# A group-normalised displaced convolution: sums as four lane tiles inside the row products, matrices written in place, one TensorE loop

## The chip, the cores and the metric

One core of one Trainium2 chip. The time is device microseconds of one execution. An execution under the profiler gives the trace; it took 1213.86 us, of which the trace's span, from the first to the last instruction, is 1212.0 us. The TensorE clock granted over it was 0.996 of full speed.

## The reference

The input x is [32 images, 384 channels, 64, 64] in float32. It is normalised over groups of 12 channels of one image, and each channel is then displaced by whole pixels and convolved with a 5x5 Gaussian of its own sub-pixel shift; 48 positions of 8 channels share an offset. The result is added to x:

```
gn(v): g = v.reshape(B, 32, 12, H, W); (g - mean(g)) / sqrt(var(g) + 1e-5)
disp = gn(x) shifted by round(offset[p]), zeros outside
kw   = exp(-|d + (offset - round(offset))|^2 / 0.5) on 5x5, normalised to sum 1
out  = x + conv_depthwise(disp, kw, padding=2)
```

Shift and Gaussian are separable, so one position is two 64x64 matrices: ay over rows and ax over columns.

## The kernel before, in words

The 384 channels are 16 superblocks of 24 channels (two groups, three positions of eight). A superblock is 16 steps of two images; a step holds 2 x 24 planes. On the 128 partitions lie four lanes of 32: each lane is one channel of a set of four, and its 32 partitions are 16 blocks of 4 rows for each of the 2 images. There are 256 steps, in 128 pairs.

Per step:

- SyncE loads the step into one of 16 slots of `xin` once the slot's old result is stored.
- VectorE takes statistics (L444, six per pair), GpSimd turns them into summands (L260, L262), TensorE multiplies them by a matrix of ones to sum over partitions (L599, `sum_stats`, once per pair), VectorE reduces the sums (L451, `sums`), and GpSimd makes the coefficients rstd and bias (L277 to L288). This runs two pairs (LEAD) ahead of the use.
- ACT (L543) and GpSimd (L297) normalise half of a step each into `norm`, double buffered.
- TensorE makes the row products (L607, `y_product`): for each of the 3 positions and 4 rows, four concurrent products of 32x128 tiles, one per lane, into PSUM. `ps` has two halves v of four banks; a lane has its bank, and columns 0 to 383 of it are used.
- ACT copies them out of PSUM into `y` (L552).
- TensorE makes the column products (L618, `x_products`) of 64x64 tiles, back into the same half of `ps`.
- VectorE adds them to `xin` (L463 and L466), and ACT issues the two stores (L569) two steps later.

In float32 a matmul of the program appears in the trace as two loads and two matmuls.

The order of the work is written out by hand for each engine. On TensorE a pair is `two_steps` (L629): row products of the even step for positions 1 and 2 (position 0 was begun at the end of the last pair, `begin_even`, L624), row products of the odd step, column products of the even step, the sums of pair p+2 into columns 384 and up of bank 3 of half 0, column products of the odd step, and position 0 of the next even step. It is a loop over 126 pairs (L674); the last two pairs follow as written-out code (L676) without sums. The other engines run `step` for the first superblock as written-out code, a loop over 14, and the last written out again.

The matrices of the next superblock are made during the current one: distances on GpSimd (L235, L241), squares and exponentials on ACT (L522, L526), the mask on VectorE (L418, `values`, at step 11), then `next_ay` by ACT in two strided activations of 768 elements (L533, at step 13) and `next_ax` by GpSimd (L249, at step 12). VectorE copies `next_ay` into `ay` ahead of the adds of step 14, once all row products of the superblock are done (`swap_rows`, L423: three copies), and `next_ax` into `ax` in step 15 (`swap_columns`, L430).

Semaphores count steps: a wait of TensorE for `norm0_ready`, `y_ready`, `result0_ready` and so on asks for a step's number, which is the loop's register `one` plus 0, 1 or 2.

Of the kernel before, what the change touches and what calls it, by code (L numbers as in the profile page):

```python
# [11 lines left out]
P = 128  # L12
# [33 lines left out]
def displaced_conv(nc: bass.Bass, x: bass.AP, offset: bass.AP, out: bass.AP):  # L46
# [7 lines left out]
    with ExitStack() as ctx:  # L54
# [25 lines left out]
        next_ay = sb("next_ay", [P, POS, R, P])  # L80
# [42 lines left out]
        next_ax = sb("next_ax", [P, POS, HW])  # L123
# [39 lines left out]
        next_ax_ready = sem("next_ax_ready")  # L163
        next_ay_ready = sem("next_ay_ready")
# [45 lines left out]
        def _(pool):  # L210
# [34 lines left out]
            def column_matrices(c):  # L245
                pool.wait_ge(made, c + 1)
                if c is not 0:
                    pool.wait_ge(ax_ready, STEPS * c)
                pool.tensor_tensor(next_ax[:], t_msk[:, :, R, :],  # L249
                                   gain[:, bass.ds(POS * c, POS)].unsqueeze(2).to_broadcast([P, POS, HW]),  # L250
                                   ALU.mult).then_inc(next_ax_ready, 1)
# [58 lines left out]
            coefficients(1, 1, early=True, used=False)  # L310

            def step(c, s, head, tail):
# [3 lines left out]
                if not (tail and s // PAIR + LEAD >= STEPS // PAIR):  # L316
# [14 lines left out]
        def _(dve):  # L331
# [80 lines left out]
            def values(c):  # L412

                dve.wait_ge(exp_ready, c + 1)
                if c is not 0:
                    dve.wait_ge(next_ax_ready, c)
                    dve.wait_ge(next_ay_ready, B * c)
# [4 lines left out]

            def swap_rows(c):  # L423
                if c is not 0:
                    dve.wait_ge(y_done, STEPS * c)
                dve.wait_ge(next_ay_ready, B * (c + 1))  # L426
                for k in range(POS):
                    nc.vector.tensor_copy(ay[:, k], next_ay[:, k]).then_inc(mats_ready[k], STEPS)  # L428

            def swap_columns(c):  # L430
                dve.wait_ge(next_ax_ready, c + 1)
                if c is not 0:
                    dve.wait_ge(x_done, ADDS * STEPS * c)
                nc.vector.tensor_copy(ax[:], next_ax[:]).then_inc(ax_ready, STEPS)
# [12 lines left out]
            def sums(pair, v, early=False, read=False):  # L447
# [27 lines left out]
            nc.vector.engine_nop().then_inc(result1_ready, SPARE)  # L475
# [8 lines left out]
            swap_columns(0)  # L484
            swap_rows(0)
            sums(1, 1, early=True)
            for s in range(2 * PAIR, AHEAD):
                all_statistics(s)

            def step(c, s, head, tail):  # L490
                t, p = STEPS * c + s, STEPS // PAIR * c + s // PAIR
                if s == STEPS - PAIR and not tail:
                    swap_rows(c + 1)
                for part in range(ADDS):
                    add_x(t, s, part)
                if s % PAIR == 0:
                    if not (tail and s // PAIR + LEAD >= STEPS // PAIR):
                        sums(p + LEAD, (s // PAIR + LEAD) % 2, read=True)
                else:
                    if s == STEPS - 1 and not tail:  # L500
                        swap_columns(c + 1)
                    if not (tail and s + AHEAD >= STEPS):
                        for f in (s - 1 + AHEAD, s + AHEAD):
                            statistics(c + f // STEPS, f % STEPS, 0, p + AHEAD // PAIR if f % PAIR == 0 else None)
                            statistics(c + f // STEPS, f % STEPS, 1)
                            statistics(c + f // STEPS, f % STEPS, 2)
# [5 lines left out]
        def _(act):  # L512
# [15 lines left out]
            def fill_rows(c, part):  # L528
                if part == 0:
                    act.wait_ge(made, c + 1)  # L530
                    if c is not 0:
                        act.wait_ge(mats_ready[POS - 1], STEPS * c)
                nc.scalar.activation(next_ay[:].rearrange("p n r (m b) -> p n (r m) b", b=B)[:, :, :, part],  # L533
                                     t_msk[:, :, 0:R].rearrange("p n r m -> p n (r m)"), ACT.Identity,
                                     scale=same[:, part:part + 1]).then_inc(next_ay_ready, 1)
# [24 lines left out]
            for part in range(B):  # L560
                fill_rows(0, part)
            for s in range(PAIR):
                normalise(s, s, 0, True)
# [7 lines left out]
            def step(c, s, head, tail):  # L571
# [4 lines left out]
                elif not head:  # L576
                    store(c - 1, s - BEHIND + STEPS, t - BEHIND)
                if not (tail and s + PAIR >= STEPS):
                    normalise(t + PAIR, (s + PAIR) % STEPS, STEPS // PAIR * c + (s + PAIR) // PAIR, False)
                if not tail:  # L580
# [6 lines left out]
                    if s == 13:  # L587
                        for part in range(B):
                            fill_rows(c + 1, part)
            run(step)  # L590
            for s in range(STEPS - BEHIND, STEPS):
# [3 lines left out]
        def _(pe):  # L595


            def sum_stats():
                nc.tensor.matmul(ps[:, 0, 3, SUMS], ones[:, :],  # L599
                                 summands[:].rearrange("p t n s -> p (t n s)"),  # L600
                                 start=True, stop=True).then_inc(stat_summed, 1)
# [27 lines left out]
            def two_steps(one, more=True, last=False):  # L629

                two, three = one + 1, one + 2
                if not isinstance(one, int):
                    two, three = pe.snap(two), pe.snap(three)
# [24 lines left out]
                if not last:  # L658

                    pe.wait_ge(result0_ready, two)  # L660
                    pe.wait_ge(result1_ready, two)
                    if more:
                        pe.wait_ge(sums_ready, one)
                    begin_even(three)
# [34 lines left out]
```

## Time and profile before

| | |
|---|---|
| median of 3 runs | 1213.13 us (1212.42 to 1213.94) |
| profiled execution | 1213.86 us |
| its span | 1212.0 us |
| TensorE busy, matmuls | 1168.3 us, 96% |
| VectorE busy | 995.4 us, 82% |
| ACT busy | 697.8 us, 58% |
| GpSimd busy | 661.0 us, 55% |
| HBM read and written | 402.7 MB, 332 GB/s over the span |

Busy time is the sum over an engine's instructions, and matmuls overlap, so 96% does not say how well TensorE is used; it says that it hardly ever has nothing in it. For the order of events the timeline is the view: each row has a start, a length, an engine and a line of the code. The chain of waits tells which engine the end hung on.

### The profile page before, as it was taken

How to read it: one execution, taken by the hardware profiler on the slowest of the kernel's cores; microseconds unless marked ns; L12 is line 12 of the kernel's file. 1: busy time of each engine (PE TensorE's matmuls, PEld its weight loads, DVE VectorE, ACT ScalarE, POOL GpSimd, SP SyncE). 2: the span in 40 equal slices, each digit the busy share in tenths (PEclk: the TensorE clock that was granted, in tenths of full speed). 3: DMA queues.
4: the chain of work that ended last, by engine and by line, in shares of the span. 5: the costliest groups of instructions: out<-in, count | busy, mean ns of one | idle time of the engine just before them, and what ended most of it. 6: DMA issues, size and time to landing. Idle time of an engine off the chain costs nothing.

```text
span 1212.0 us, 110760 instructions
## 1 busy us (share of the span) xinstructions
PE 1168.3 (96%) x49408; PEld 1126.2 (93%) x49408; DVE 995.4 (82%) x1530; ACT 697.8 (58%) x595; POOL 661.0 (55%) x1478
## 2 busy tenths in 40 slices
PE   2999999999999999999999999999999999999996
PEld 2899999999999999999999999999999999999996
DVE  7688887887888888788888888888888888878863
ACT  3466656656556555655656655565665665556553
POOL 5455656455565555555556555555655556565551
PEclk9999999999999999999999999999999999999999
DMA  6999999999999999999999999999999999999955
GB/s 210 333 356 349 346 347 345 344 339 350 337 347 346 335 351 346 341 346 344 344 340 350 341 337 348 348 343 341 345 348 341 343 343 346 347 339 346 330 182 185
DMA packets 409765, 403.01 MB, mean 333 GB/s; under 512 B 16528, under 2 KB 409744, under 8 KB 409744
## 3 DMA queue, kind: packets, MB, share of 16 engines
q1 hardware_dynamic: 204944, 201.41, 50.9%
q10 hardware_dynamic: 204800, 201.36, 49.6%
q8 instruction: 9, 0.15, 0.1%
q14 instruction: 12, 0.10, 0.0%
HBM read 201.38 MB, written 201.33 MB: 332 GB/s over the span
## 4 chain that ended last, share of the span: by engine, by line
PE 94%; DVE 3%; issue 2%; POOL 1%; DVEq 0%; POOLq 0%
PE ps L607 59%; PE ps L618 31%; PE ps L599 4%; DVE ay L428 1%; DVE xin L463 1%; DVE stats L444 0%; POOL norm L297 0%; POOL t_int L235 0%; POOL t_full L241 0%; POOL grid_i L215 0%; DVE xin L466 0%; POOL var L284 0%; POOL rstd L286 0%; DVEq L426 0%; DVE sub L382 0%
## 5 line engine op out<-in xcount | busy, mean ns | idle before, releaser
L607 PE MATMUL ps<-ay,norm 32*128 32x128 f32 x24576 | 728.9, 273 | 0.7 <-DVE both L451 0.3
L607 PEld LDWEIGHTS ps<-ay,norm 32*128 32x128 f32 x24576 | 705.4, 187 | 10.5 <-DVE both L451 0.5
L552 ACT ACTIVATE y<-ps 128x1536 f32<-128x1536 f32 x256 | 369.9, 1445 | 418.4 <-PE ps L607 418.1
L444 DVE BATCH_NORM_STATS2 stats<-xin 128x6 f32<-128x512 f32 x768 | 475.7, 691 | 0.1
L618 PE MATMUL ps<-ax,y 64*64 64x64 f32 x24576 | 417.7, 220 | 6.2 <-issue 6.0
L618 PEld LDWEIGHTS ps<-ax,y 64*64 64x64 f32 x24576 | 382.4, 135 | 27.8 <-issue 6.8
L297 POOL TENSOR_SCALAR norm<-xin,rstd,bias 128x768 f32<-128x768 f32 x256 | 264.1, 1032 | 211.3 <-PE ps L607 187.6
L466 DVE TENSOR_TENSOR xin<-ps,xin 128x1024 f32<-128x1024 f32 x256 | 312.9, 1222 | 44.2 <-PE ps L618 44.0
L543 ACT ACTIVATE norm<-xin,bias,rstd 128x768 f32<-128x768 f32 x256 | 263.0, 1028 | 72.3 <-issue 72.2
L463 DVE TENSOR_TENSOR xin<-ps,xin 128x512 f32<-128x512 f32 x256 | 175.7, 686 | 148.3 <-PE ps L618 148.3
L277 POOL TENSOR_TENSOR mean_sq<-both 128x4 f32<-128x4 f32 x128 | 25.5, 199 | 215.1 <-DVE both L451 196.6
L286 POOL TENSOR_TENSOR rstd<-var,mhalf 128x4 f32<-128x4 f32 x128 | 129.2, 1009 | 10.0
L599 PE MATMUL ps<-summands,ones 128*128 128x36 f32 x256 | 49.4, 277 | 30.6 <-POOL summands L262 23.2
L599 PEld LDWEIGHTS ps<-summands,ones 128*128 128x128 f32 x256 | 38.5, 190 | 41.2 <-issue 32.3
L262 POOL TENSOR_TENSOR summands<-stats 128x12 f32<-128x12 f32 x128 | 27.3, 213 | 20.9 <-POOL summands L260 20.8
L235 POOL TENSOR_TENSOR t_int<-grid,place 128x960 f32<-128x960 f32 x16 | 28.7, 1796 | 7.1 <-DVEq L398 7.0
L284 POOL TENSOR_TENSOR var<-spread,mean_sq 128x4 f32<-128x4 f32 x128 | 26.4, 206 | 10.0
L282 POOL TENSOR_TENSOR spread<-inner,both 128x4 f32<-128x4 f32 x128 | 25.8, 202 | 10.7
L533 ACT ACTIVATE next_ay<-t_msk,same 128x768 f32<-128x768 f32 x32 | 30.2, 1000 | 1.8 <-DVE t_msk L418 1.8
L288 POOL TENSOR_TENSOR bias<-minus_mean,rstd 128x4 f32<-128x4 f32 x128 | 25.5, 199 | 10.0
L279 POOL TENSOR_SCALAR inner<-both 128x4 f32<-128x4 f32 x128 | 25.4, 199 | 10.1
L241 POOL TENSOR_TENSOR t_full<-t_int,sub 128x960 f32<-128x960 f32 x16 | 28.7, 1797 | 0.1
(54 smaller groups left out, 188.4 us busy)
## 6 DMA issues: line engine op xcount, KB each, us to landing
xin<-in_x_dram SPq DMA_DIRECT2D x512, 384.0 KB, 5.6
out_dram<-xin ACTq DMA_DIRECT2D x512, 384.0 KB, 6.1
off<-in_L_conv_offset_dram SPq DMA_DIRECT2D x1, 48.0 KB, 3.2
```

The costliest lines, as they stand in the source:

```text
L235: pool.tensor_tensor(t_int[:], grid[:, None, :, :].to_broadcast([P, POS, KINDS, HW]), place[:, bass.ds(POS * c, POS), :].unsqueeze(3).to_b ...
L286: pool.tensor_tensor(rstd[:, v], var[:, v], mhalf[:, :], ALU.pow).then_inc(small, 1)
L297: pool.tensor_scalar(norm[:, s % 2, :, cols].rearrange("p r (q w) -> p q r w", w=HW), xin[:, s, QG:].rearrange("p q (r w) -> p q r w", w=H ...
L444: nc.vector.bn_stats(stats[:, s // PAIR % RING, s % PAIR, n, :], xin[:, s].rearrange("p (g q) f -> p q f g", g=GROUPS)[:, n]).then_inc(bn_ ...
L463: nc.vector.tensor_tensor(at, ps[:, s % 2, 2:4, 0:ROW], at, ALU.add).then_inc(result0_ready, 1)
L466: nc.vector.tensor_tensor(at, ps[:, s % 2, 0:2].rearrange("p h (k f) -> p h k f", k=2), at, ALU.add).then_inc(result1_ready, 1)
L533: nc.scalar.activation(next_ay[:].rearrange("p n r (m b) -> p n (r m) b", b=B)[:, :, :, part], t_msk[:, :, 0:R].rearrange("p n r m -> p n ...
L543: nc.scalar.activation(norm[:, s % 2, :, cols].rearrange("p r (q w) -> p q r w", w=HW), xin[:, s, 0:QG].rearrange("p q (r w) -> p q r w", ...
L552: nc.scalar.activation(y[:, v].rearrange("p k r a m -> p a (k r) m"), ps[:, v, :, 0:POS * P].rearrange("p a (n m) -> p a n m", m=32), ACT. ...
L599: nc.tensor.matmul(ps[:, 0, 3, SUMS], ones[:, :], summands[:].rearrange("p t n s -> p (t n s)"), start=True, stop=True).then_inc(stat_summ ...
L607: last = nc.tensor.matmul(ps[:, v, a, P * k:P * (k + 1)], norm[rows, v, r, P * k:P * (k + 1)], ay[rows, k, r, :], start=(r == 0), stop=(r ...
L618: last = nc.tensor.matmul(ps[outs, v, 2 * (k // 2) + h, at:at + HW], y[rows, v, k, r].rearrange("p a m -> p (a m)")[:, outs], ax[rows, k], ...
```

## The change

Four things change.

1. The sums. `sum_stats` becomes four products, one per lane of 32 rows, each into columns 384 and up of its lane's bank, and moves: in the pair it now stands in the even step, between positions 1 and 2. VectorE's `sums` adds the four lanes too (144 values in place of 36), after the even step's copy of y, placed before the last of the six statistics of the odd step. TensorE waits for it before the even column products, which overwrite those columns. `make_summands` moves behind `coefficients` in the odd step and works for a pair one further ahead.
2. The matrices. `next_ay`, `next_ax` and VectorE's copies go. ACT writes `ay` directly in step 15, behind its copy of y and the stores, as six activations (two per position); GpSimd writes `ax` directly at the end of step 15, after all column products of the superblock.
3. TensorE's loop runs over all 128 pairs. So the last two pairs have sums as well, and a surplus row product of position 0 follows the last pair. ACT and VectorE raise the semaphores it needs.
4. The start: TensorE begins the first even step after the first sums; the sums of pair 1 follow behind position 0 and those of pair 2 inside the first pair of the loop. ACT puts the first fills of `ay` between its two normalises.

The core of the diff:

```diff
@@ pool
-                if c is not 0:
-                    pool.wait_ge(ax_ready, STEPS * c)
-                pool.tensor_tensor(next_ax[:], t_msk[:, :, R, :],
+                if c is not 0:
+                    pool.wait_ge(x_done, ADDS * STEPS * c)
+                pool.tensor_tensor(ax[:], t_msk[:, :, R, :],
...
-                    if s % PAIR == 0:
-                        make_summands(p + LEAD, (s // PAIR + LEAD) % RING)
-                    else:
-                        coefficients(p + LEAD, (s // PAIR + LEAD) % 2)
+                if s % PAIR == 1:
+                    if not (tail and s // PAIR + LEAD >= STEPS // PAIR):
+                        coefficients(p + LEAD, (s // PAIR + LEAD) % 2)
+                    if not (tail and s // PAIR + LEAD + 1 >= STEPS // PAIR):
+                        make_summands(p + LEAD + 1, (s // PAIR + LEAD + 1) % RING)
...
-                    if s == 12:
+                    if s == STEPS - 1:
                         column_matrices(c + 1)
@@ vector
-            def swap_rows(c):
-            def swap_columns(c):
...
+                if evicted is not None:
+                    dve.wait_ge(y_ready, evicted)
                 ready = nc.vector.tensor_reduce(
                     both[:, v].rearrange("p (t g) f -> p t (g f)", t=PAIR),
-                    ps[:, 0, 3, SUMS].rearrange("p (t n e) -> p t e n", t=PAIR, n=CHUNKS), AX.X, ALU.add)
+                    ps[:, pair if early else 0, :, SUMS].rearrange("p a (t n e) -> p t e a n", t=PAIR, n=CHUNKS),
+                    AX.XY, ALU.add)
...
+            def pair_statistics(c, s, p, reduced):
+                for f in (s, s + 1):
+                    for part in range(CHUNKS):
+                        if reduced and f > s and part == CHUNKS - 1:
+                            reduced()
+                        statistics(c + f // STEPS, f % STEPS, part, p if f == s and part == 0 else None)
...
+                        def reduced():
+                            sums(p + LEAD + 1, (s // PAIR + LEAD + 1) % 2, read=True, evicted=t + PAIR)
@@ scalar
+            def fill_rows(c, k):
+                if k == 0:
                     act.wait_ge(made, c + 1)
+                for part in range(B):
+                    filled_k = nc.scalar.activation(ay[:, k].rearrange("p r (m b) -> p (r m) b", b=B)[:, :, part],
+                                                    t_msk[:, k, 0:R].rearrange("p r m -> p (r m)"), ACT.Identity,
+                                                    scale=same[:, part:part + 1])
+                filled_k.then_inc(mats_ready[k], STEPS)
...
+                if s == STEPS - 1 and not tail:
+                    for k in range(POS):
+                        fill_rows(c + 1, k)
@@ tensor
+            def sum_stats(v):
+                for a in range(LANES):
+                    rows = slice(32 * a, 32 * a + 32)
+                    last = nc.tensor.matmul(ps[:, v, a, SUMS], ones[rows, :],
+                                            summands[rows].rearrange("p t n s -> p (t n s)"), start=True, stop=True)
+                last.then_inc(stat_summed, 1)
...
                 pe.wait_ge(mats_ready[1], one)
                 y_product(1, 0)
+                pe.wait_ge(summands_ready, one)
+                sum_stats(0)
                 pe.wait_ge(mats_ready[2], one)
                 y_product(2, 0)
...
                 pe.wait_ge(ax_ready, one)
+                pe.wait_ge(sums_ready, one)
                 pe.wait_ge(y_ready, one)
                 pe.sem_inc(x_started, 1)
                 x_products(0)
-                if more:
-                    pe.wait_ge(summands_ready, one)
-                    pe.wait_ge(result0_ready, two)
-                    sum_stats()
                 pe.wait_ge(y_ready, two)
                 pe.sem_inc(x_started, 1)
                 x_products(1)
...
-            sum_stats()
+            sum_stats(0)
             pe.wait_ge(first_sums, 1)
+            begin_even(1)
             pe.wait_ge(first_summands, 2)
-            sum_stats()
-            pe.wait_ge(first_sums, 2)
-            begin_even(1)
-            with pe.Fori(1, PAIR * (PAIRS - LEAD) + 1, PAIR) as one:
+            sum_stats(1)
+            with pe.Fori(1, TOTAL + 1, PAIR) as one:
                 two_steps(one)
-            for p in range(PAIRS - LEAD, PAIRS):
-                two_steps(PAIR * p + 1, more=False, last=p == PAIRS - 1)
```

## Rows read from the trace of the kernel before

**Rows 1.** The chain of work that ended last, by line, as shares of the span.

```profile
PE ps L607 59%; PE ps L618 31%; PE ps L599 4%; DVE ay L428 1%; DVE xin L463 1%; DVE stats L444 0%; POOL norm L297 0%; POOL t_int L235 0%; POOL t_full L241 0%; POOL grid_i L215 0%; DVE xin L466 0%; POOL var L284 0%; POOL rstd L286 0%; DVEq L426 0%; DVE sub L382 0%
```

**Rows 2.** Groups by line and form: busy us, mean ns of one, idle before and releaser.

```profile
L607 PEld LDWEIGHTS ps<-ay,norm 32*128 32x128 f32 x24576 | 705.4, 187 | 10.5 <-DVE both L451 0.5 <-issue 0.3
L618 PEld LDWEIGHTS ps<-ax,y 64*64 64x64 f32 x24576 | 382.4, 135 | 27.8 <-issue 6.8
L599 PEld LDWEIGHTS ps<-summands,ones 128*128 128x128 f32 x256 | 38.5, 190 | 41.2 <-issue 32.3
L533 ACT ACTIVATE next_ay<-t_msk,same 128x768 f32<-128x768 f32 x32 | 30.2, 1000 | 1.8 <-DVE t_msk L418 1.8
L451 DVE TENSOR_REDUCE both<-ps 128x12 f32<-128x36 f32 x128 | 23.6, 185 | 0.6 <-PE ps L599 0.6
```

**Rows 3.** Timeline of an ordinary pair: start us, length us, engine, line.

```profile
588.91 0.20 POOL L277 TENSOR_TENSOR mean_sq<-both 128x4 f32<-128x4 f32 x1 [1.96 <-DVE both L451]
...
589.17 5.64 PE L607 MATMUL ps<-ay,norm 32*128 32x128 f32 x192
...
591.27 0.20 POOL L288 TENSOR_TENSOR bias<-minus_mean,rstd 128x4 f32<-128x4 f32 x1
592.27 1.45 ACT L552 ACTIVATE y<-ps 128x1536 f32<-128x1536 f32 x1 [2.79 <-PE ps L607]
...
593.69 0.21 POOL L262 TENSOR_TENSOR summands<-stats 128x12 f32<-128x12 f32 x1 [0.15 <-POOL summands L260]
...
594.74 1.49 PEld L618 LDWEIGHTS ps<-ax,y 64*64 64x64 f32 x96
...
594.97 1.43 ACT L552 ACTIVATE y<-ps 128x1536 f32<-128x1536 f32 x1
595.05 0.98 POOL L297 TENSOR_SCALAR norm<-xin,rstd,bias 128x768 f32<-128x768 f32 x1 [1.15 <-PE ps L607]
...
596.31 0.30 PEld L599 LDWEIGHTS ps<-summands,ones 128*128 128x128 f32 x2
...
596.65 1.63 PE L618 MATMUL ps<-ax,y 64*64 64x64 f32 x96
...
598.21 2.05 PE L607 MATMUL ps<-ay,norm 32*128 32x128 f32 x61
```

**Rows 4.** Timeline of the column stage at a superblock's end.

```profile
612.86 1.63 PE L618 MATMUL ps<-ax,y 64*64 64x64 f32 x96
613.14 1.10 DVE L428 COPY ay<-next_ay 128x512 f32<-128x512 f32 x3 [0.88 <-PE ps L607]
613.16 1.43 ACT L552 ACTIVATE y<-ps 128x1536 f32<-128x1536 f32 x1
...
615.30 1.63 PE L618 MATMUL ps<-ax,y 64*64 64x64 f32 x96
```

**Rows 5.** The waits: total us, times, longest us.

```profile
PE ps L599 <- DVE xin L463: 7.4, 15, 0.5
```

**Rows 6.** Timeline of the last two pairs, behind TensorE's loop.

```profile
1189.40 2.66 PE L618 MATMUL ps<-ax,y 64*64 64x64 f32 x143
1189.54 1.45 ACT L552 ACTIVATE y<-ps 128x1536 f32<-128x1536 f32 x1 [0.20 <-PE ps L607]
...
1191.11 0.82 PEld L618 LDWEIGHTS ps<-ax,y 64*64 64x64 f32 x48 [0.21 <-issue]
...
1193.48 0.93 PE L618 MATMUL ps<-ax,y 64*64 64x64 f32 x49 [1.42 <-issue]
...
1204.80 1.03 PE L618 MATMUL ps<-ax,y 64*64 64x64 f32 x52 [1.64 <-issue]
```

**Rows 7.** Timeline of the start.

```profile
24.65 7.31 DVE L444 BATCH_NORM_STATS2 stats<-xin 128x6 f32<-128x512 f32 x12
...
24.78 7.46 PE L607 MATMUL ps<-ay,norm 32*128 32x128 f32 x192 [0.35 <-DVE both L451]
...
38.05 0.92 PE L618 MATMUL ps<-ax,y 64*64 64x64 f32 x44 [2.94 <-issue]
```

More of the change, by code:

```diff
@@ L315, in step @@
                     normalise(t + PAIR, (s + PAIR) % STEPS, STEPS // PAIR * c + (s + PAIR) // PAIR)
-                if not (tail and s // PAIR + LEAD >= STEPS // PAIR):
-                    if s % PAIR == 0:
-                        make_summands(p + LEAD, (s // PAIR + LEAD) % RING)
+                if s % PAIR == 1:
[3 more added lines that the diff above has]
+                        make_summands(p + LEAD + 1, (s // PAIR + LEAD + 1) % RING)
                     else:
-                        coefficients(p + LEAD, (s // PAIR + LEAD) % 2)
+                        pool.engine_nop().then_inc(summands_ready, PAIR)
                 if not tail:
@@ L445, in statistics, with sums @@
                                    xin[:, s].rearrange("p (g q) f -> p q f g", g=GROUPS)[:, n]).then_inc(bn_done, 1)
-            def sums(pair, v, early=False, read=False):
+            def sums(pair, v, early=False, read=False, evicted=None):
                 if read:
@@ L483, in _ @@
             all_statistics(3)
-            swap_columns(0)
-            swap_rows(0)
             sums(1, 1, early=True)
-            for s in range(2 * PAIR, AHEAD):
-                all_statistics(s)
+            nc.vector.engine_nop().then_inc(result1_ready, SPARE)
+            def pair_statistics(c, s, p, reduced):
[4 more added lines that the diff above has]
+                        statistics(c + f // STEPS, f % STEPS, part, p if f == s and part == 0 else None)
+            pair_statistics(0, 4, None, None)
+            pair_statistics(0, 6, None, lambda: sums(LEAD, LEAD % 2, read=True, evicted=1))
             def step(c, s, head, tail):
                 t, p = STEPS * c + s, STEPS // PAIR * c + s // PAIR
-                if s == STEPS - PAIR and not tail:
-                    swap_rows(c + 1)
                 for part in range(ADDS):
                     add_x(t, s, part)
-                if s % PAIR == 0:
-                    if not (tail and s // PAIR + LEAD >= STEPS // PAIR):
-                        sums(p + LEAD, (s // PAIR + LEAD) % 2, read=True)
-                else:
-                    if s == STEPS - 1 and not tail:
-                        swap_columns(c + 1)
+                if s % PAIR == 1:
+                    reduced = None
+                    if not (tail and s // PAIR + LEAD + 1 >= STEPS // PAIR):
+                        def reduced():
+                            sums(p + LEAD + 1, (s // PAIR + LEAD + 1) % 2, read=True, evicted=t + PAIR)
+                    else:
+                        nc.vector.engine_nop().then_inc(sums_ready, PAIR)
                     if not (tail and s + AHEAD >= STEPS):
[L503 to L506, printed above, removed]
+                        pair_statistics(c, s - 1 + AHEAD, p + AHEAD // PAIR, reduced)
+                    elif reduced:
+                        reduced()
                     if s == 11 and not tail:
@@ L559, in _ @@
             act.wait_ge(filled, FILLS)
[L560 to L563, printed above, removed]
+            fill_rows(0, 0)
+            normalise(0, 0, 0, True)
+            fill_rows(0, 1)
+            fill_rows(0, 2)
+            normalise(1, 1, 0, True)
             def store(c, s, t):
@@ L586, in step @@
                         exponential(c + 1)
-                    if s == 13:
-                        for part in range(B):
-                            fill_rows(c + 1, part)
             run(step)
+            act.wait_ge(norm0_ready, TOTAL)
+            act.sem_inc(norm0_ready, 1)
+            act.wait_ge(mats_ready[0], TOTAL)
+            act.sem_inc(mats_ready[0], 1)
             for s in range(STEPS - BEHIND, STEPS):
@@ L627, in begin_even, with two_steps @@
                 y_product(0, 0)
[L629 to L633, printed above, removed]
+            def two_steps(one):
+                two, three = pe.snap(one + 1), pe.snap(one + 2)
                 pe.wait_ge(norm1_ready, one)
@@ L657, in two_steps @@
                 x_products(1)
[L658 to L664, printed above, removed]
+                pe.wait_ge(result0_ready, two)
+                pe.wait_ge(result1_ready, two)
+                begin_even(three)
             pe.wait_ge(filled, FILLS)
             pe.wait_ge(first_summands, 1)
-            sum_stats()
+            sum_stats(0)
             pe.wait_ge(first_sums, 1)
+            begin_even(1)
             pe.wait_ge(first_summands, 2)
-            sum_stats()
-            pe.wait_ge(first_sums, 2)
-            begin_even(1)
-            with pe.Fori(1, PAIR * (PAIRS - LEAD) + 1, PAIR) as one:
+            sum_stats(1)
+            with pe.Fori(1, TOTAL + 1, PAIR) as one:
                 two_steps(one)
-            for p in range(PAIRS - LEAD, PAIRS):
-                two_steps(PAIR * p + 1, more=False, last=p == PAIRS - 1)
 _INS = ["x", "L0_conv_offset"]
```

31 lines of the change are left out of this document (4 added, 27 removed).

## The prediction

> **What bounds the kernel now.** I read the chain of waits first: of the work that ended last, 59% lies on L607 (the row products), 31% on L618 (the column products) and 4% on L599 (the sums) [rows 1]. TensorE (PE) sets the end, so an edit is worth what it does to TensorE's own order of work and nothing else, until another engine makes it wait. Then I read the timeline of one ordinary pair of steps [rows 3]. The row products of a pair start at 589.17 and again at 598.21, a period of 9.04 us; it holds the row products of both steps (589.17 to 594.74, 5.57 us), the column products of the even step, the two sum matmuls, the column products of the odd step (594.74 to 596.65 to 598.21: 1.91 and 1.56 us). 128 such periods are the time. Last I looked for the periods that are not ordinary: the end of each superblock [rows 4, 5], the end [rows 6] and the start [rows 7].
>
> **The sums on TensorE.** Before, one 128x128 product in two passes stands between the two column stages. The stage with it takes 1.91 us, the one without it 1.56, so it costs 0.35 us [rows 3]. After, it is four products over 32 rows each, in two passes: 8 loads and 8 matmuls of the row products' own form, between position 1 and position 2 of the even step.
>
> What they cost there: a load of 128 columns is busy 187 ns and one of 64 columns 135 ns [rows 2]; 64 columns more cost 52 ns, so 128 columns take about 105 ns of the loading path. The two loads of the old sums (189 ns each, 0.30 us together) start 0.11 us apart although only 36 columns move behind each [rows 2, 3]. The row products run 192 loads in 5.57 us, 48 sets of four lanes, 0.116 us a set [rows 3]. All three say that a set of four 128-column loads takes 0.11 us whatever moves behind it. Two sets: +0.22 us per pair. Bounds: 0.12 (twice the column products' pace of 24 sets in 1.49 us [rows 3], whose loads are half as wide) and 0.35 (what the sums cost now). The Trainium skill, "TensorE: Matmul & The Clock Gate", section on LDWEIGHTS, speaks against the change here: a load costs by its columns, and one of 32 rows takes as long as one of 128. The trace agrees, by the 52 ns above.
>
> What comes back between the column stages: not 0.35 us. The odd step's column products also wait for its copy of y out of PSUM (L552). ACT starts it 0.23 us after the even column products start, and it takes 1.43 us: it ends 1.66 after them [rows 3], when the sums still hide it. At a superblock's end it starts 0.30 after them [rows 4]; over the loop I take 0.25. How soon TensorE follows is seen once, in the first pair after the loop, which has no sums: copy at 1189.54 for 1.45 us, so to 1190.99, and the first load at 1191.11, 0.12 us later [rows 6]. So the new distance is 0.25 + 1.43 + 0.13 = 1.81 in place of 1.91: 0.10 us saved. The copy can't start sooner: ACT runs copy, two store issues, normalise, copy, 2.70 us from 592.27 to 594.97 [rows 3], about as long as the row products of one step (half of 5.57), and both copies move by the same 0.22. Bounds of the saving: 0.03 and 0.20 (1.91 less the 1.71 of [rows 6]). The Trainium skill, "TensorEngine Tiling (Array Packing)", section "Key Properties", says that a change of tiling mode drains TensorE; by that alone the whole 0.35 us would return. It is the third rival.
>
> An ordinary pair is thus longer by 0.22 - 0.10 = 0.12 us. There are 126 pairs in the loop, 15 of them at a superblock's end: 111 x 0.12 = +13.3 us.
>
> **Matrices in place.** At a superblock's end VectorE copies ay in three pieces (1.10 us) ahead of its adds, TensorE waits for the add before the sums, and the stage takes 615.30 - 612.86 = 2.44 us [rows 4]; 15 such waits, 7.4 us [rows 5]. The copies and this wait go. The stage becomes 0.30 + 1.43 + 0.12 = 1.85, say 1.84: 0.60 saved, 0.22 added, 15 x -0.38 = -5.7 us.
>
> What is late next: ACT writes ay itself, after the last row products have been copied. In that step its order is copy, store issues, six activations of 256 elements, normalise, copy. The old fill of 768 elements takes 1.00 us [rows 2]; two of 256 I put at 0.9 us (bounds 0.67, by elements, and 2.0, two full ones). The copy ends 1.7 us after the column products start and the store issues a little later; I put ACT free at 1.9, position 0 is ready at 2.8 us, and the row products that read it start at 1.84 + 1.56 = 3.4. Positions 1 and 2 follow at 3.7 and 4.6, wanted at 4.3 and 5.4. The normalise behind them ends at 5.7, wanted at 6.3. All hidden by 0.6 us or more; at the upper bound the first would be 0.5 us late, 15 times. On GpSimd the column matrix now waits for the end of all column products; behind it stands only the next normalise, due 3 us later. Cost 0.
>
> **The longer route of the sums.** GpSimd, in the odd step: normalise until 1.3 us after the column stage starts (595.05 plus 0.98, less 594.74), coefficients 2.56 us (588.91 to 591.27 plus 0.20), summands 0.6 (two operations like that at 593.69, with a wait between) [rows 3]: ready at 4.5. TensorE wants them at 3.37 + 16 sets of 0.11 = 5.2. VectorE then waits for the even copy (y stage + 3.3 + 1.45) and reduces 144 values in place of 36: 0.185 us now [rows 2], at most four times that; I take 0.35 (lower bound 0.185). It is done 5.2 us into the row products, where TensorE asks for it at 5.8. Hidden by 0.6 us; at 0.74 us still hidden by 0.2. One statistic (0.7 us) stands behind it and then the adds, which start 0.7 us after the column products. Cost 0.
>
> **End.** The last two pairs were written out behind the loop and wait there for nothing that the trace shows: 1.42 us at 1193.48, 1.64 at 1204.80 [rows 6]. In the loop they should not: -3.1 us (bounds 0 and -4). They now carry sums: +0.44. The surplus row product at the very end runs beside the last adds and stores: 0.
>
> **Start.** The first row products begin at about 21.8 instead of 24.78 [rows 7]: they wait for the first coefficients only. But the sums of pair 2 stand inside the first even step, and VectorE reads steps 4 and 5 only from 24.65 on, six statistics: 28.4, summands at 29.0. TensorE has nothing to do from about 25.5 to 29.1, where before it ran through. Position 2 and the odd step follow: the first column products come at 33.5 to 35 against 32.2. The idle time of 2.94 us ahead of 38.05 [rows 7] I leave as it is. I take +2.5 us (bounds -3, if the early start survives or the gap covers the later one, and +5).
>
> **Sum.** 13.3 - 5.7 - 3.1 + 0.4 + 2.5 = +7.4 us. The profiled execution took 1213.86 (span 1212.0), 0.7 above the median of 1213.13; on the profile it gives 1221.3, on the median 1220.5.
>
> **Rivals.**
> 1. *The loads of the four lanes hide, and it is faster.* If a set costs only by its 36 moving columns, two sets are 0.12 us or less. Then 111 x 0.02 - 15 x 0.48 + 0.2 - 3.1 + 2.5 = -5.4: 1207.7; at no cost at all -20.7: 1192.4. For it: no change of form on either side of the sums. Against: the 0.11 us between the two old loads. It decides below 0.16 us for both sets. Chance 0.22.
> 2. *The sums' route becomes the bound.* The reduction or the summands come after TensorE asks for them. Margin 0.6 us at both; passed by 0.2 us in each of 126 pairs it is +25: 1246. For it: three engines in a row now hang on one even copy. Against: VectorE is idle before its adds today. With it goes the milder form, ay late by 0.5 at 15 ends: 1228. Chance 0.12.
> 3. *The whole drain comes back.* The column stages touch at 1.56 us: -0.13 x 111 - 0.66 x 15 + 0.4 - 3.1 + 2.5 = -24.5: 1188.6. Against it stands the wait of [rows 6]. Chance 0.03.
> 4. *The edits cancel.* A set at 0.09 us and a good start: within 2.4 us of before. Chance 0.11.
>
> The forecast has 0.52. About 0.2% (2.4 us) is what a measurement of this kernel can tell from no change. Slower: 0.52 less its lowest corner, plus rival 2, 0.62; no change 0.14; faster, rivals 1 and 3 with a little of the low corner, 0.24. Range of the forecast alone 1214 to 1229; 8 in 10, with most of the upper part of rival 1: 1203 to 1230.
>
> **What would show it.** Right: the period of an ordinary pair 9.14 to 9.20 us; the row products of a pair 5.8 us, with eight 32x128 sum loads that add 0.22; TensorE idle 0.1 to 0.25 us before the odd column products, ended by ACT's copy; no long period at a superblock's end; no idle of TensorE in the last two pairs; a gap of 3 us or more near 26 us. Wrong: a pair under 9.07 (loads hidden), TensorE waiting on VectorE's reduction or on GpSimd's summands in the steady part (rival 2), or row products that wait for ACT at a superblock's start.

## The result, and the profile after

The changed kernel takes 1223.15 us (median of 4 runs, 1222.26 to 1225.63) against 1213.54 before (4 runs). The ratio is 1.0083, 95% interval 1.0065 to 1.0101: slower by 9.6 us, clear of the noise. 7.4 us more were forecast, 1220.5.

In the rows below, PE is TensorE with its matmuls, PEld its loads of the stationary operand (for the sums the matrix of ones); the moving operand (the summands, 36 columns) passes behind each load. DVE is VectorE, POOL GpSimd. In brackets stands the idle time of the engine ahead of a row and what ended it.

The chain of waits of the changed kernel; before, TensorE held nearly all of it [rows 1]:

```profile
PE ps L611 60%; PE ps L622 20%; ACT y L548 12%; PE ps L603 2%; ACTq L566 0%; ACTq L547 0%; DVE xin L457 0%; DVEq L54 0%; ACTq L564 0%; ACT ay L528 0%; DVE xin L454 0%; ACTq L179 0%; ACTq L526 0%
```

A new member has come in: ACT's copy of y (L548), with 12%. It takes its share from the column products (L622, 31% before), because the chain now goes through the copy and not through the column products beside it. The waits name the same thing (total us, times, longest us):

```profile
DVE both L441 <- ACT y L548: 68.8, 126, 3.5
...
PE ps L622 <- ACT y L548: 22.2, 106, 0.5
```

No such row of TensorE was there before. The wait of TensorE for an add at a superblock's end [rows 5] is gone. VectorE's reduction waits for ACT's copy in nearly every pair, 68.8 us in all, and TensorE doesn't wait for the reduction in the steady pairs.

The groups (busy us, mean ns of one, idle before):

```profile
L441 DVE TENSOR_REDUCE both<-ps 128x12 f32<-128x144 f32 x128 | 39.5, 308 | 71.2 <-ACT y L548 68.8
...
L603 PEld LDWEIGHTS ps<-summands,ones 32*128 32x128 f32 x1040 | 44.9, 190 | 19.7 <-issue 16.1
L528 ACT ACTIVATE ay<-t_msk,same 128x256 f32<-128x256 f32 x96 | 41.2, 521 | 6.1 <-issue 4.2
```

The load of 32 rows and 128 columns takes 190 ns, the old one of 128 rows took 190 [rows 2]. The reduction of four times the values takes 0.31 us, not four times as long.

The timeline of an ordinary pair, the answer to [rows 3]:

```profile
588.92 2.09 PE L611 MATMUL ps<-ay,norm 32*128 32x128 f32 x64
...
589.79 0.21 POOL L258 TENSOR_TENSOR summands<-stats 128x12 f32<-128x12 f32 x1 [0.15 <-POOL summands L256]
...
590.70 0.34 PEld L603 LDWEIGHTS ps<-summands,ones 32*128 32x128 f32 x8
...
590.95 3.85 PE L611 MATMUL ps<-ay,norm 32*128 32x128 f32 x128
592.26 1.45 ACT L548 ACTIVATE y<-ps 128x1536 f32<-128x1536 f32 x1 [2.83 <-PE ps L611]
...
593.81 0.31 DVE L441 TENSOR_REDUCE both<-ps 128x12 f32<-128x144 f32 x1 [0.52 <-ACT y L548]
594.02 1.03 ACT L539 ACTIVATE norm<-xin,bias,rstd 128x768 f32<-128x768 f32 x1 [0.31 <-issue]
...
594.73 1.63 PE L622 MATMUL ps<-ax,y 64*64 64x64 f32 x96
594.96 1.44 ACT L548 ACTIVATE y<-ps 128x1536 f32<-128x1536 f32 x1
...
596.54 1.63 PE L622 MATMUL ps<-ax,y 64*64 64x64 f32 x96 [0.18 <-ACT y L548]
596.58 1.23 DVE L457 TENSOR_TENSOR xin<-ps,xin 128x1024 f32<-128x1024 f32 x1 [0.40 <-PE ps L622]
...
598.16 2.07 PE L611 MATMUL ps<-ay,norm 32*128 32x128 f32 x64
```

Row products with the sums in them: 594.73 - 588.92 = 5.81 us (5.57 before). Column stages 596.54 - 594.73 = 1.81 us apart (1.91 before), and the last 0.18 of it TensorE is idle until the copy of y, 594.96 plus 1.44, has ended. The next row products start at 598.16, 0.35 us after the end of VectorE's add (596.58 plus 1.23 is 597.81). In 33 of the pairs 3 to 126 the row products are late, in nearly all by less than 0.1 us, and start this same 0.35 us after the add of the even step.

From the starts in both traces, over pairs 3 to 126: row products of a pair 5.595 before and 5.808 after, +0.213 us; column stages 1.977 apart before (in the median 1.913 in ordinary pairs, 2.439 at a superblock's end) and 1.825 after, -0.152; odd column stage to the next row products 1.575 and 1.585, +0.010. That is a mean period of 9.147 and 9.219: an ordinary pair went from 9.089 to 9.210 (+0.121), one at a superblock's end from 9.574 to 9.285 (-0.289). Over these 124 pairs it makes 26.4 - 18.8 + 1.2 = +8.8 us.

A superblock's end, the answer to [rows 4]:

```profile
622.36 1.63 PE L622 MATMUL ps<-ax,y 64*64 64x64 f32 x96
622.66 1.43 ACT L548 ACTIVATE y<-ps 128x1536 f32<-128x1536 f32 x1
...
624.23 1.63 PE L622 MATMUL ps<-ax,y 64*64 64x64 f32 x96 [0.25 <-ACT y L548]
...
624.36 2.58 ACT L528 ACTIVATE ay<-t_msk,same 128x256 f32<-128x256 f32 x6 [0.27 <-issue]
...
625.79 2.09 PE L611 MATMUL ps<-ay,norm 32*128 32x128 f32 x64
```

The stage takes 1.87 us in place of 2.44, and the six activations into `ay` start 2.0 us after the even column products and are done after 4.6, as they had been put. The row products do not wait for them.

The end, where TensorE's idle times of [rows 6] stood, and the start, which answers to [rows 7]:

```profile
1206.24 2.09 PE L611 MATMUL ps<-ay,norm 32*128 32x128 f32 x64
1208.13 0.34 PE L603 MATMUL ps<-summands,ones 32*128 32x36 f32 x8
1208.27 3.85 PE L611 MATMUL ps<-ay,norm 32*128 32x128 f32 x128
1212.05 3.35 PE L622 MATMUL ps<-ax,y 64*64 64x64 f32 x192
```

```profile
21.90 2.09 PE L611 MATMUL ps<-ay,norm 32*128 32x128 f32 x32 [5.07 <-ACT norm L539]
...
29.43 0.43 PE L603 MATMUL ps<-summands,ones 32*128 32x36 f32 x8 [2.99 <-POOL summands L258]
...
41.08 1.98 PE L622 MATMUL ps<-ax,y 64*64 64x64 f32 x62 [3.52 <-issue]
```

From the row products of pair 127 to the last column matmul TensorE needed 21.8 us before and 18.1 after: -3.7. The row products of the third pair begin at 53.96 in place of 49.54: +4.4. With +8.8 for the pairs between and +0.3 behind the last matmul the sum is +9.8, and the spans differ by 9.9 (1212.0 and 1221.9).

### The profile page after: what moved, and what is told of

It is laid out like the page before. It is cut to its first block, busy times and chain, and to the rows that moved or that the text cites. A ratio compares the mean times of both kernels' runs of the same rounds, so it can differ in the third digit from the quotient of the medians.

```text
span 1221.9 us, 112479 instructions
## 1 busy us (share of the span) xinstructions
PE 1163.0 (95%) x50224; PEld 1122.9 (92%) x50224; DVE 1000.0 (82%) x1466; ACT 706.5 (58%) x659; POOL 659.1 (54%) x1478
## 4 chain that ended last, share of the span: by engine, by line
PE 81%; ACT 12%; issue 3%; ACTq 1%; DVE 0%; DVEq 0%
PE ps L611 60%; PE ps L622 20%; ACT y L548 12%; PE ps L603 2%; ACTq L566 0%; ACTq L547 0%; DVE xin L457 0%; DVEq L54 0%; ACTq L564 0%; ACT ay L528 0%; DVE xin L454 0%; ACTq L179 0%; ACTq L526 0%
## 5 line engine op out<-in xcount | busy, mean ns | idle before, releaser
L611 PE MATMUL ps<-ay,norm 32*128 32x128 f32 x24608 | 759.2, 275 | 6.1 <-ACT norm L539 5.1
L611 PEld LDWEIGHTS ps<-ay,norm 32*128 32x128 f32 x24608 | 721.8, 188 | 16.1 <-issue 6.4
L548 ACT ACTIVATE y<-ps 128x1536 f32<-128x1536 f32 x256 | 369.4, 1443 | 416.7 <-PE ps L611 416.6
L431 DVE BATCH_NORM_STATS2 stats<-xin 128x6 f32<-128x512 f32 x768 | 487.0, 690 | 0.1
L622 PE MATMUL ps<-ax,y 64*64 64x64 f32 x24576 | 417.9, 220 | 28.3 <-ACT y L548 22.2
L622 PEld LDWEIGHTS ps<-ax,y 64*64 64x64 f32 x24576 | 386.3, 135 | 57.8 <-issue 42.3
L441 DVE TENSOR_REDUCE both<-ps 128x12 f32<-128x144 f32 x128 | 39.5, 308 | 71.2 <-ACT y L548 68.8
L603 PE MATMUL ps<-summands,ones 32*128 32x36 f32 x1040 | 46.0, 237 | 19.2 <-POOL summands L258 19.2
L603 PEld LDWEIGHTS ps<-summands,ones 32*128 32x128 f32 x1040 | 44.9, 190 | 19.7 <-issue 16.1
L528 ACT ACTIVATE ay<-t_msk,same 128x256 f32<-128x256 f32 x96 | 41.2, 521 | 6.1 <-issue 4.2
L280 POOL TENSOR_TENSOR var<-spread,mean_sq 128x4 f32<-128x4 f32 x128 | 26.4, 206 | 10.0
L256 POOL TENSOR_SCALAR summands<-stats 128x24 f32<-128x24 f32 x128 | 27.6, 216 | 5.8 <-DVE stats L431 1.4
```

Of the source, the lines that this page charges most:

```text
L431: nc.vector.bn_stats(stats[:, s // PAIR % RING, s % PAIR, n, :], xin[:, s].rearrange("p (g q) f -> p q f g", g=GROUPS)[:, n]).then_inc(bn_ ...
L441: ready = nc.vector.tensor_reduce(both[:, v].rearrange("p (t g) f -> p t (g f)", t=PAIR), ps[:, pair if early else 0, :, SUMS].rearrange(" ...
L528: filled_k = nc.scalar.activation(ay[:, k].rearrange("p r (m b) -> p (r m) b", b=B)[:, :, part], t_msk[:, k, 0:R].rearrange("p r m -> p (r ...
L548: nc.scalar.activation(y[:, v].rearrange("p k r a m -> p a (k r) m"), ps[:, v, :, 0:POS * P].rearrange("p a (n m) -> p a n m", m=32), ACT. ...
L603: last = nc.tensor.matmul(ps[:, v, a, SUMS], ones[rows, :], summands[rows].rearrange("p t n s -> p (t n s)"), start=True, stop=True)
L611: last = nc.tensor.matmul(ps[:, v, a, P * k:P * (k + 1)], norm[rows, v, r, P * k:P * (k + 1)], ay[rows, k, r, :], start=(r == 0), stop=(r ...
```

## The experiments

Each was compared with runs of the kernel before on its own chip, whose medians were 1213.5 to 1213.9 us.

**1. The sums back, the rest kept.** `e1_sums_back` has the matrices in place and one loop of 128 pairs, but the sums, their queue order and TensorE's start of the kernel before:

```diff
                 pe.wait_ge(mats_ready[1], one)
                 y_product(1, 0)
-                pe.wait_ge(summands_ready, one)
-                sum_stats(0)
                 pe.wait_ge(mats_ready[2], one)
...
                 x_products(0)
+                pe.wait_ge(summands_ready, one)
+                pe.wait_ge(result0_ready, two)
+                sum_stats()                       # one 128x128 product, bank 3
                 pe.wait_ge(y_ready, two)
```

> Parts 2 and 3 alone: matrices in place and one loop of 128 pairs, but the sums as before (one 128x128 product between the column stages, one pair later in the queue of GpSimd and VectorE as before) and the start of before. Theory (the four lane tiles are what costs time, the other parts save): ordinary pair 9.07 us, no 2.44 us column stage at a superblock's end (15 x 0.5 = 7 us saved), last two pairs 3 us shorter: 1202 to 1204 us. Rival (the matrices in place or the single loop cost time, and the sums are neutral): 1213 or more, with long periods at a superblock's end.

Measured: 1202.0 us, ratio 0.9899 (0.9882 to 0.9915). Column stages are 1.91 to 1.93 us apart at every position of a superblock, the last too, and the mean period is 9.080. The last two pairs take TensorE 18.1 us, as in the changed kernel, and not the 21.8 of before. So the two other parts save 11.8 us, and what the sums and their route do to the pairs and the start costs 21 us more than that against the changed kernel (1223.15 - 1202.0). By the traces 17.2 us of it are the pairs (124 x 0.139) and 3.7 the start. The rival falls.

**2. Each sum made twice.** The changed kernel with the four products repeated at once in the same place (`for again in range(2)` around the lanes).

> The changed kernel with each sum made twice in the same place, 16 loads and 16 matmuls of 32 rows in place of 8. Theory (0.11 us for each set of four lanes): row products of a pair 5.81 + 0.21 = 6.02 us, 128 x 0.21 = 27 us more: 1250 us. Rival (the 0.21 us is the price of going over to the sums and back, a wait or the first load, not of the products): 5.81 to 5.9 us, 1223 to 1235 us.

Measured: 1251.49 us, ratio 1.0314 (1.0297 to 1.0331). Row products with the sums in them, mean 6.046 us against 5.808: +0.238 for the second 8 loads, +0.213 for the first 8. Eight loads are two sets, a set being four loads side by side, one per lane: 0.107 to 0.119 us a set. It is the products themselves that cost.

**3. Wide moving data.** The changed kernel with 128 moving columns behind each load:

```diff
-        summands = sb("summands", [P, PAIR, CHUNKS, 3 * GROUPS])
+        wide = sb("wide", [P, P])        # zeros; the first 36 columns are the summands
...
-                    last = nc.tensor.matmul(ps[:, v, a, SUMS], ones[rows, :],
-                                            summands[rows].rearrange("p t n s -> p (t n s)"), start=True, stop=True)
+                    last = nc.tensor.matmul(ps[:, v, a, POS * P:4 * P], ones[rows, :], wide[rows, :],
+                                            start=True, stop=True)
```

> The changed kernel with 128 moving columns behind each load of the sums in place of 36 (the other 92 are zeros and land in unused columns). Theory (the loads of 128 columns set the pace, not what moves): row products of a pair stay at 5.81 to 5.83 us, 1223 us. Rival (the moving columns or the end of the small matmuls set the cost): 0.05 to 0.15 us more per pair, 1230 to 1242 us.

Measured: 1223.08 us, ratio 1.0076 (1.0059 to 1.0093), the time of the changed kernel with 36 columns. The timeline of its TensorE:

```profile
595.78 2.08 PE L614 MATMUL ps<-ay,norm 32*128 32x128 f32 x64
597.67 0.42 PE L606 MATMUL ps<-wide,ones 32*128 32x128 f32 x8
597.90 3.77 PE L614 MATMUL ps<-ay,norm 32*128 32x128 f32 x128
601.60 0.62 PE L625 MATMUL ps<-ax,y 64*64 64x64 f32 x25
```

601.60 - 595.78 = 5.82 us, as before. Three and a half times the moving columns are free behind a load of 128 columns. With experiment 2 this settles the first rival: the loads set the cost. It is not their number: in the column products a set of as many loads, of 64 columns each, takes 0.06 us (24 sets in 1.49).

**4. The old form at the new place.** One 128x128 product between the row products:

```diff
-                for a in range(LANES):
-                    rows = slice(32 * a, 32 * a + 32)
-                    last = nc.tensor.matmul(ps[:, v, a, SUMS], ones[rows, :], ...
+                nc.tensor.matmul(ps[:, v, 3, SUMS], ones[:, :],
+                                 summands[:].rearrange("p t n s -> p (t n s)"), start=True, stop=True)
```

> The changed kernel with the sums as one 128x128 product (two loads, two matmuls, one bank for VectorE) at their new place inside the row products. Theory (the form costs time only where it differs from its neighbours: going to 128x128 and back costs 0.13 us or more beside 0.22 for the two loads): row products of a pair 5.95 to 6.05 us, 1241 to 1254 us. Rival (no price for the change of form, the loads alone count): 5.81 us, 1223 us.

Measured: 1269.04 us, ratio 1.0462 (1.0442 to 1.0481), 15 us above the range that was expected.

```profile
590.11 2.09 PE L609 MATMUL ps<-ay,norm 32*128 32x128 f32 x64
592.12 0.41 PE L601 MATMUL ps<-summands,ones 128*128 128x36 f32 x2
592.47 3.85 PE L609 MATMUL ps<-ay,norm 32*128 32x128 f32 x128
596.25 1.63 PE L620 MATMUL ps<-ax,y 64*64 64x64 f32 x96
```

The first 64 row matmuls take 2.01 us until the sums start, and 1.9 when four lane tiles follow. In all the row products take 6.148 us, 0.553 above the 5.595 without sums. Two loads 0.11 us apart are 0.22 of it, so 0.33 us are left for the change to this form and back. It had been put at 0.13, from the stage between the column products. The Trainium skill ("TensorEngine Tiling (Array Packing)", "Key Properties") says that changing mode drains TensorE, and the trace agrees, by these 0.33 us; the size depends on the neighbours. So the lane tiles are the right form for this place. It is the place that is dear: nothing there hides them.

**5. Four 64x64 tiles between the column products.** As experiment 1, with the sums in the column products' own form:

```diff
-                nc.tensor.matmul(ps[:, 0, 3, SUMS], ones[:, :],
-                                 summands[:].rearrange("p t n s -> p (t n s)"),
-                                 start=True, stop=True).then_inc(stat_summed, 1)
+                pe.sem_inc(sum_started, 1)
+                for h, m in ((0, 0), (1, 0), (0, 1), (1, 1)):
+                    rows, outs = slice(64 * h, 64 * h + 64), slice(64 * m, 64 * m + 64)
+                    last = nc.tensor.matmul(ps[outs, 0, 2 + h, SUMS], ones[rows, outs],
+                                            summands[rows].rearrange("p t n s -> p (t n s)"), start=True, stop=True)
+                last.then_inc(stat_summed, 1)
```

VectorE adds banks 2 and 3. Nothing waits for `sum_started`.

> As e1_sums_back, but the sums are four 64x64 tile products (two row halves, two column halves) between the column stages, the same form as the column products, two banks for VectorE to add. Theory (a set costs by its 64 columns, 0.06 us, two sets 0.12; and the odd column products wait for ACT's copy of y until about 1.81 us after the even ones in any case): the sums vanish in that wait, column stages 1.81 us apart, ordinary pair 8.97, 1190 to 1192 us. Rival (the change of form costs nothing, the place between the column stages costs 0.35 whatever the form): 1.91 us apart, 1202 to 1204 us. Rival 2 (no wait for the copy): 1.68 apart, pair 8.84, 1175 us.

Measured: 1199.77 us, ratio 0.9883 (0.9860 to 0.9906), 8 us above what the theory gave. The column stages are 1.825 us apart on average, as the theory had it, but the gain was handed back behind them: the row products begin 1.656 us after the odd column products in place of 1.574. The timeline of one such pair:

```profile
709.41 1.63 PE L607 MATMUL ps<-ax,y 64*64 64x64 f32 x96
...
710.50 0.22 DVE L437 TENSOR_REDUCE both<-ps 128x12 f32<-128x72 f32 x1
...
711.08 2.16 PE L596 MATMUL ps<-ay,norm 32*128 32x128 f32 x65
```

The reduction ends at 710.72, and the row products start 0.36 us later. TensorE's queue had two more waits to work off after the one for the sums, those of `begin_even`. In 102 of 124 pairs the row products are late and this distance is 0.35 us. The kernel before has the same order of waits and the same 0.35 us, but there the reduction comes late in 22 pairs only, and by little.

**6. The order of TensorE's waits.** As experiment 5, with the waits ahead of the row products turned round (`begin_even` is the waits for `norm0_ready` and `mats_ready[0]` and then `y_product(0, 0)`):

```diff
+                pe.wait_ge(norm0_ready, three)
+                pe.wait_ge(mats_ready[0], three)
                 pe.wait_ge(result0_ready, two)
                 pe.wait_ge(result1_ready, two)
                 pe.wait_ge(sums_ready, one)
-                begin_even(three)
+                y_product(0, 0)
```

> e2_quad64 with TensorE's wait for VectorE's sums as the last wait ahead of the next row products (there it stood ahead of the waits for the normalised data and the matrix). In e2 the row products began up to 0.2 us late, 0.3 us after the reduction's end. Theory (TensorE's queue spent about 0.2 us on the waits behind that one): row products 1.56 to 1.60 us after the odd column products start instead of 1.66, 8 to 12 us less: 1188 to 1192 us. Rival (the reduction itself comes too late, or the store and load traffic, now at 350 GB/s, holds the pace): 1198 to 1200 us.

Measured: 1187.22 us, ratio 0.9782 (0.9764 to 0.9800). The odd column products and the next row products are 1.564 us apart again, and the mean period is 8.984 us against 9.087. Where the reduction comes late, the row products now start as little as 0.15 us after its end. The waits are the same, and only the one that is met last now stands last: 12.6 us, on two chips with nearly the same time of the kernel before (1213.82 and 1213.47), and 12.8 by the traces (124 x 0.103).

**7. The 64x64 tiles twice.** As experiment 6, `for h, m in 2 * (...)`.

> e9_quad64_wait_order with the four 64x64 products made twice, 16 loads in place of 8. Theory (1.56 + 2 x 0.12 = 1.80 us fits into the 1.81 that ACT's copy of y sets): column stages still 1.81 to 1.83 us apart, VectorE's reduction up to 0.12 us later and so the row products by as much in some pairs: 1187 to 1195 us. Rival (the distance of 1.81 us is TensorE's own work with the sums in it, not a wait): 1.93 us apart, 128 x 0.12 = 15 us more, 1202 us.

Measured: 1190.14 us, ratio 0.9799 (0.9781 to 0.9817).

```profile
594.49 1.63 PE L607 MATMUL ps<-ax,y 64*64 64x64 f32 x96
596.05 0.44 PE L588 MATMUL ps<-summands,ones 64*64 64x36 f32 x16
596.30 1.66 PE L607 MATMUL ps<-ax,y 64*64 64x64 f32 x96
```

596.30 - 594.49 = 1.81 us again, with 16 loads in it in place of 8; the mean is 1.832 against 1.826, the mean period 8.990 against 8.984. The second set of products is hidden, so in experiment 6 the distance is a wait for the copy of y and not TensorE's work; here the work, 1.56 + 0.25, just fills it. Of the 3 us that the whole kernel is slower, 2 stand at the start: its third pair begins at 49.28 and that of experiment 6 at 47.33. Starts differ by that much without a reason in the code: in experiments 3 and 9 (the first kernel) TensorE has the order of the changed kernel at the start, and their third pairs begin at 51.68 and 51.37, against its 53.96.

**8. Two products of 64 rows and 128 columns there.** As experiment 6, `ones[rows, :]` for each half of the rows.

> e9_quad64_wait_order with the sums as two products of 64 rows and 128 columns (two sets of loads of 128 columns) in place of four 64x64 products. Theory (a set costs by its columns, and a form unlike the neighbours' costs 0.13 us or more on top): column stages 1.56 + 0.22 + 0.13 = 1.91 us apart or more, 0.1 us a pair above e9 or more: 1199 to 1203 us. Rival (whatever stands there hides in the wait for the copy of y): 1187 us as e9.

Measured: 1197.54 us, ratio 0.9861 (0.9844 to 0.9878); column stages 1.904 us apart in the median and 1.907 in the mean, the mean period 9.063, 0.08 above that of experiment 6. 1.558 is the distance with nothing between a column stage and the next stage. Of the 0.35 us above it, 0.22 are the two sets of 128 columns, and 0.13 are left for the change of form. In experiment 7, with four sets in the neighbours' form, nothing was left beside the sets themselves (1.56 + 4 x 0.06 = 1.80 of 1.81).

**9. ACT's stores behind its normalise,** in the changed kernel and in experiment 6 (the four lines that call `store` moved behind `normalise`).

> The changed kernel with ACT's store issues moved behind its normalise in each step. Theory (the odd column products start when ACT's copy of y is done, and that copy starts 0.23 to 0.33 us after the even ones because ACT comes late from the store issues of the even step): the copy starts 0.13 after them, the column stages lie 1.71 apart in place of 1.82, 126 x 0.11 = 14 us less: 1209 to 1212 us. Rival (the 0.25 us ahead of the odd column products is TensorE's own, or the copy is held by something else): 1.82, 1223 us.

> e9_quad64_wait_order with ACT's store issues behind its normalise. Theory: the column stages move from 1.82 to 1.71 us apart, but VectorE's reduction, which is tied to the even column products, then holds the row products: 3.3 us after the even column products in place of 3.4, 3 to 10 us less than e9. Rival (the reduction already holds them in e9): no difference from e9.

Measured: 1220.28 us, ratio 1.0061 (1.0040 to 1.0081), and 1185.47 us, ratio 0.9765 (0.9747 to 0.9782). They gain 2.9 and 1.8 us, where 11 to 14 and 3 to 10 were expected: both theories fall. The intervals overlap with those without the edit; the traces show 0.020 us a pair in both. The timeline of the first:

```profile
590.55 1.63 PE L622 MATMUL ps<-ax,y 64*64 64x64 f32 x96
590.75 1.45 ACT L548 ACTIVATE y<-ps 128x1536 f32<-128x1536 f32 x1 [0.32 <-PE ps L611]
```

ACT is now idle for 0.32 us before its copy, and yet the copy starts 0.20 us after the column products. The mean went from 0.246 to 0.201 us, because the late ones (0.27 to 0.35 at three positions of a superblock) became 0.21; the ordinary 0.23 became 0.21 too. So the stores and the normalise did hold the ordinary start: in the changed kernel the normalise runs from 594.02 to 595.05 and the copy follows at 594.96 without idle time. But they held it only 0.02 us longer than the next thing would have. And of the 0.028 us by which the column stages came closer, 0.011 were lost again behind them: VectorE's add, with its 0.35 us, now holds the row products in 45 pairs in place of 33. In ACT's written-out first and last superblocks it is 0.13 to 0.16 in all these kernels, inside ACT's loop no less than 0.2. What ACT's queue does there in the 0.08 us was not tried.

The version of experiment 6, with or without the late stores, beats both kernels, by 2.2% (without) and 2.35% (with) against the kernel before. The difference between these two versions is within their intervals.

## Why the prediction was right

By its own steps:

- *The sums on TensorE,* +0.22 us a pair: +0.213 in the trace. That the loads and not the moving columns set it: experiments 2 and 3.
- *What comes back between the column stages,* 0.10 us a pair because the odd column products wait for the copy of y: 1.913 to 1.81 in ordinary pairs. That it is this wait: the profile's row, and experiment 7. One reason given for it was only half of it: the copy "can't start sooner" since ACT's chain of 2.70 us holds it. With the chain loosened (experiment 9) the copy comes 0.02 us sooner at five positions of eight and 0.06 to 0.14 at three; then it follows the end of TensorE's row products, and starts 0.2 us after the column products do.
- *Matrices in place,* 15 x 0.60 saved: 2.439 to 1.875 in the median, 0.56 each. Such a pair became 0.29 us shorter in all, where 0.38 was put; the rest is 0.04 us more behind its odd column products. TensorE waits for `ay` once, for 0.2 us, and never for `ax`, and `ay` is ready when it was said. Experiment 1 shows the saving without the new sums.
- *The longer route of the sums,* cost 0. In the pair shown the summands are ready at 590.00 and TensorE comes for them at 590.70; the reduction ends at 594.12, wanted at 594.73. Margins 0.7 and 0.6 us, as given. What was not foreseen are 0.010 us a pair more behind the odd column products, most of them where VectorE's add of the even step ends 0.35 us ahead of the row products. The column stages lie closer, and the add, which ends some 3.0 us after the even column products start, is now the next thing that holds TensorE.
- *End,* -3.1 us and +0.4 for the sums, -2.7 together: -3.7. Experiment 1 has the same end. The last written-out pair also ran its row products slower (6.21 us in place of 5.63), which was left out of the term.
- *Start,* +2.5 us: +4.4. The gap before the sums of pair 2 is there, 2.99 us where 3.6 was put, and the first column products come at 35.06, at the upper end of the 33.5 to 35 given. But the later idle time, taken as unchanged, grew from 2.94 to 3.52 us, and the row products after it were slow for longer. This term was mis-sized most, but with the same order at the start experiments 3 and 9 have +2.1 and +1.8, so +2.5 lies within what one kernel's start does, and the 1.9 us by which it was missed say little.

An ordinary pair was put at +0.12 us and measured +0.121, though its period is 9.21 and not within the 9.14 to 9.20 given: the 9.04 read before was that of a short pair, the mean there is 9.09. The sum of the first three terms, +7.6, met +8.8 for the same pairs; the difference lies at the superblocks' ends. The start was put 1.9 us too low and the end 0.7 too high (1.0 less the 0.3 behind the last matmul), which partly cancel; the whole came out 2.2 us short. The second rival (the sums' route as the bound) and the third (the whole drain comes back) did not come. The third came near in experiment 6 by another way: the change of form was avoided and the products fitted into a wait.

## What to carry to other kernels

A product on TensorE that has a few moving columns costs its load; ask first where in TensorE's order there is a wait that could hold it, and give it the form of its neighbours there. The dear thing about the old sums, 0.35 us, was worth 0.10 only, as a wait of 0.25 us lay under it: before moving work off a place, look at what else ends there. Behind one wait stands the next: here VectorE's add took back a part of what closer column stages gave. Where an engine waits for several signals, put the one that comes last at the end.

## What the runs showed of the hardware

- A set of loads of 128 columns takes 0.107 to 0.12 us of TensorE with 36 or with 128 moving columns behind it, for tiles of 32 rows (experiments 2 and 3); sets of 64 columns in the 64x64 form take 0.06 (four in 0.25, experiment 7).
- Changing the form and back costs 0.33 us for one 128x128 product inside 32x128 products (experiment 4), and 0.13 for one inside 64x64 products (experiment 1: 1.91 less 1.56) or for two 64x128 products there (experiment 8). These are rests, after 0.22 us for two sets of loads.
- With two waits still to work off after the one that was met last, TensorE starts 0.35 us after VectorE's end (experiment 5), with none 0.15 (experiment 6): some 0.1 us for each, if both cost the same. The order of five waits was worth 12.6 us in 128 pairs.
- Written-out code behind a loop cost TensorE 3.7 us in two pairs against two more rounds of the loop (21.8 us before, 18.1 in the changed kernel and in experiment 1). Why was not tried.
